# Silu of the expert gates as one ScalarE instruction, in an attention and expert block

## The reference

```python
h = _layernorm(x) * (1 + ca) + sa
x = x + ga * attention(h)                 # 16 heads, causal, content part 16 wide, rotary part 64 wide
h = _layernorm(x) * (1 + cb) + sb
# the experts, on h as x:
probs = softmax(x @ gate_weight.T)        # 32 experts
top_val, top_idx = top_k(probs, 8); top_val /= sum(top_val)
w_tg = weights of the top 8, summed by merge group (8 groups)
gate, up = split(einsum('th,goh->tgo', x, gate_up_proj[dominant_experts]))   # 96 wide for each group
act = jax.nn.silu(gate) * up
y = einsum('tgi,ghi->tgh', act, down_proj[dominant_experts])
out = einsum('tg,tgh->th', w_tg, y)
x = x + gb * out
```

## Time and profile before

| | |
|---|---|
| median of 3 runs | 1019.88 us (1019.28 to 1020.67) |
| the profiled execution | 1020.3 us, of which its span is 1018.6 |
| mean granted TensorE clock | 0.981 |
| PE busy | 962.8 us (95%) |
| PE weight loads busy | 704.9 us (69%) |
| DVE busy | 685.2 us (67%) |
| POOL busy | 496.8 us (49%) |
| ACT busy | 426.2 us (42%) |

### The profile page before, as it was taken

How to read it: one execution, slowest core, us unless ns; L and a number is a source line. 1 busy time by engine, 2 the same in 40 slices (tenths; PEclk the granted TensorE clock), 3 DMA queues, 4 the chain that set the end, 5 groups by cost and what they waited for, 6 DMA issues and landing times.

```text
span 1018.6 us, 23971 instructions
## 1 busy us (share of the span) xinstructions
PE 962.8 (95%) x9847; PEld 704.9 (69%) x9847; DVE 685.2 (67%) x1371; ACT 426.2 (42%) x780; POOL 496.8 (49%) x462
## 2 busy tenths in 40 slices
PE   5789999999999999999999999999999999998897
PEld 3546667766687677866777667866778667875566
DVE  5676767675776757667676758777576766766334
ACT  5234444264433634344442644245443445333332
POOL 2345454673545552663625644555526636356202
PEclk9889999999999999999999999999999999999999
DMA  6322010210102101200102101030002101011000
GB/s 205 81 87 84 33 62 2 75 63 2 63 1 95 43 11 53 73 33 33 63 2 73 64 2 63 7 99 33 33 33 73 49 17 63 1 53 64 2 1 21
DMA packets 37599, 48.73 MB, mean 48 GB/s; under 512 B 9386, under 2 KB 23210, under 8 KB 37490
## 3 DMA queue, kind: packets, MB, share of 16 engines
q1 hardware_dynamic: 37490, 47.20, 13.9%
HBM read 17.80 MB, written 4.21 MB: 22 GB/s over the span
## 4 chain that ended last, share of the span: by engine, by line
PE 75%; DVE 9%; ACT 6%; POOL 4%; issue 3%; DMA 2%; SPq 2%; POOLq 0%; DVEq 0%; ACTq 0%
PE ring L1206 15%; PE ring L1053 11%; PE ring L1054 9%; PE ring L1055 9%; PE ring L1178 7%; PE av L1222 7%; ACT pt L746 3%; DVE mcol L943 3%; PE ring L1283 2%; PE ring L1285 2%; PE ring L1284 2%; DVE prod L919 2%; PE ring L1190 2%; PE ring L1114 1%; SPq L537 1%
## 5 line engine op out<-in xcount | busy, mean ns | idle before, releaser
L746 ACT ACTIVATE pt<-ring 128x384 f32<-128x384 f32 (+1 forms) x384 | 171.0, 533 | 256.7 <-PE ring L1206 226.8
L943 DVE TENSOR_REDUCE mcol<-ring 128x1 f32<-128x128 f32 (+3 forms) x512 | 211.1, 482 | 47.8 <-PE ring L1183 47.2
L624 POOL TENSOR_SCALAR_AFFINE_SELECT pt<-pt 128x512 f32<-128x512 f32 x128 | 81.0, 646 | 215.4 <-ACT pt L746 215.4
L919 DVE TENSOR_TENSOR prod<-ring,table 128x1024 f32<-128x1024 f32 x128 | 154.5, 1217 | 44.4 <-PE ring L1055 40.1
L1206 PE MATMUL ring<-rows 32*128 32x512 f32 (+3 forms) x3072 | 172.2, 329 | 6.5 <-ACT pt L746 5.3
L1206 PEld LDWEIGHTS ring<-rows 32*128 32x128 f32 x3072 | 127.4, 184 | 53.4 <-issue 20.4
L597 POOL TENSOR_TENSOR rows<-prod,rows 128x1024 fp32r<-128x1024 f32 x64 | 152.6, 2390 | 17.3 <-ACT rows L725 16.4
L590 POOL TENSOR_TENSOR prod<-prod 128x512 f32<-128x512 f32 x64 | 82.0, 1281 | 87.2 <-DVE prod L919 86.6
L1178 PE MATMUL ring<-rows 32*128 32x512 f32 (+3 forms) x1024 | 89.9, 361 | 16.3 <-DMA cont<-h_lo 4.7
L725 ACT ACTIVATE rows<-prod 128x1024 fp32r<-128x1024 f32 x64 | 67.7, 1073 | 88.0 <-POOL prod L591 83.1
L1222 PE MATMUL av<-pt,vals 128*17 128x512 f32 (+3 forms) x1024 | 87.3, 447 | 4.3 <-POOL pt L624 4.3
(11 more groups left out here) (189 smaller groups left out, 1798.5 us busy)
## 6 DMA issues: line engine op xcount, KB each, us to landing
cont<-h_hi SPq DMA_DIRECT2D x96, 128.0 KB, 2.0
cont<-h_lo SPq DMA_DIRECT2D x96, 128.0 KB, 2.0
xn<-x_dram SPq DMA_DIRECT2D x8, 512.0 KB, 4.7
xr<-x_dram SPq DMA_DIRECT2D x8, 512.0 KB, 4.2
out_dram<-xr SPq DMA_DIRECT2D x8, 512.0 KB, 3.2
gate_bc<-gates_scratch SPq DMA_DIRECT2D x8, 256.0 KB, 4.4
pt<-wmod_dram SPq DMA_DIRECT2D x1, 1536.0 KB, 6.7
pt<-gup_t_dram SPq DMA_DIRECT2D x16, 96.0 KB, 2.5
```

What stands on the lines that cost most here:

```text
L746: sc.activation(pt[:, PT_AT[n] + h * w:PT_AT[n] + (h + 1) * w], ps[:, 0:w], ACT.Exp, scale=SCALE).then_inc(exp_ready.sem, 1)
L919: ve.tensor_tensor(prod[:, s % PROD, :, :], ps[:, :].unsqueeze(1).broadcast_to([P, 2, S]), table[:, :, :], ALU.mult).then_inc(rotated.sem, 1)
L943: last = ve.reduce_max(mcol[:, q, h * HR + ONE_ROW:h * HR + ONE_ROW + 1], ps[:, at:at + (q + 1) * P], AX_X)
```

## The change

ScalarE applies silu to the bank of gate and writes it to `inner`. The VectorE step `gated` is gone with its semaphore; the bank of gate is released by ScalarE, and `upped` is a plain product. The step keeps the name `tanh`. In both written orders all six of these steps now stand behind `ex.0`, and both orders are new throughout; `SETUP_ORDER` and the numbers of warm matmuls are the same.

```diff
@@ semaphores
-        tanh_ready = Count(sem("tanh_ready"), FT)
@@ ScalarE, kind == "tanh"
                         ps = wait_full(sc, b, part, ("gate", ahead, k))
-                        sc.activation(inner[:, k, :], ps[:, :], ACT.Tanh, scale=0.5).then_inc(tanh_ready.sem, 1)
+                        sc.activation(inner[:, k, :], ps[:, :], ACT.Silu).then_inc(gate_used.sem, 1)
@@ VectorE
-                    elif kind == "gated":
-                        k = step[2]
-                        wait(ve, tanh_ready, b, ahead, k)
-                        ps, act = bank(b, part, PLACES[part][0][("gate", ahead, k)]), inner[:, k, :]
-                        ve.scalar_tensor_tensor(act, act, 1.0, ps[:, :], ALU.add, ALU.mult)\
-                          .then_inc(gate_used.sem, 1)
                     elif kind == "upped":
...
-                        ve.scalar_tensor_tensor(act, act, 0.5, ps[:, :], ALU.mult, ALU.mult)\
-                          .then_inc(up_used.sem, 1)
+                        ve.tensor_tensor(act, act, ps[:, :], ALU.mult).then_inc(up_used.sem, 1)
@@ BODY_ORDER, the start
-rope.0200 score.000 rotate.0200 load_next.1 rope.0201 exp.000 loads.0 maxima.010 rotate.0201 clear.000 qcon.01
-reduce.010 combine.020 score.001 qcon_hi.01 qcon_lo.01 rope.0210 exp.001 maxima.011 rotate.0210 clear.001 rope.0211
-reduce.011 maxima.012 rotate.0211 value.000 reduce.012 combine.021 value.001 score.002 kcon.01 exp.002 shift.01
-rope.0300 kcon_hi.01 clear.002 hi.020 kcon_lo.01 rope.0301 shifted.01 move_k.02 hi.021 lo.020 stats1.1 value.002
+score.000 load_next.1 rope.0200 exp.000 rope.0201 rotate.0200 score.001 rotate.0201 clear.000 stats1.1 combine.020
+value.000 exp.001 maxima.010 rope.0210 reduce.010 clear.001 pow1.1 score.002 rotate.0210 rope.0211 exp.002 maxima.011
+rotate.0211 clear.002 value.001 reduce.011 combine.021 maxima.012 value.002 reduce.012 kcon.01 qcon.01 kcon_hi.01
+hi.020 kcon_lo.01 shift.01 qcon_hi.01 move_k.02 lo.020 rope.0300 shifted.01 hi.021 qcon_lo.01 score.010 move_q.02
...
@@ BODY_ORDER, the middle
-pow1.1 value.010 exp.011 maxima.020 combine.030 norm1.1 rope.0311 reduce.020 score.012 clear.011 rotate.0311
-maxima.021 combine.031 exp.012 move_q.03 maxima.022 hi.030 move_k.03 reduce.021 hi.031 clear.012 turn1.10 reduce.022
-turn1.11 lo.030 modulate1.10 value.011 modulate1.11 low1.10 shift.02 maxima.030 shifted.02 low1.11 value.012
-reduce.030 score.020 attn_out.01 score.021 exp.020 maxima.031 clear.020 exp.021 value.020 reduce.031 clear.021 lo.031
+attn_out.00 rotate.0300 rope.0301 exp.010 maxima.020 rotate.0301 norm1.1 clear.010 maxima.021 reduce.020 combine.030
+value.010 reduce.021 lo.021 maxima.022 rope.0310 reduce.022 score.011 rotate.0310 rope.0311 exp.011 turn1.10
+rotate.0311 clear.011 score.012 modulate1.10 combine.031 shift.02 exp.012 move_k.03 low1.10 turn1.11 shifted.02
+value.011 hi.030 loads.0 move_q.03 score.020 clear.012 modulate1.11 lo.030 hi.031 value.012 low1.11 score.021 exp.020
+attn_out.01 maxima.030 clear.020 exp.021 value.020 reduce.030 clear.021 lo.031 score.022 maxima.031 exp.022 value.021
...
@@ BODY_ORDER, the experts
-values_out.11 up.00 logits_copy.0 turn_l.0 gate.00 top.0 rotate.1110 up.01 tanh.00 rotate.1111 ex.0 gate.01 top2.0
-gate.02 tanh.01 gated.00 turn_w.0 gated.01 up.02 wT.0 upped.00 tanh.02 upped.01 gate.03 wT_lo.0 weigh.00 weigh.01
+rotate.1111 maxima.102 logits_copy.0 hi.110 combine.111 turn_l.0 reduce.102 up.00 gate.00 top.0 ex.0 up.01 top2.0
+gate.01 tanh.00 upped.00 turn_w.0 tanh.01 up.02 wT.0 upped.01 wT_lo.0 gate.02 weigh.00 weigh.01 weighed.00 up.03
...
@@ LAST_ORDER, the attention of group 1 and 2
-... exp.010 rope.0301 kcon_lo.01 move_k.02 score.011 attn_out.00 lo.021 rope.0310 rotate.0301 exp.011 maxima.020 clear.010 value.010 rotate.0310 combine.030 reduce.020 score.012 exp.012 rope.0311 maxima.021 rotate.0311 reduce.021 maxima.022 combine.031 clear.011 hi.030 clear.012 ...
+value.001 shifted.01 score.010 hi.020 move_k.02 clear.002 hi.021 lo.020 value.002 exp.010 attn_out.00 maxima.020
+rope.0300 reduce.020 clear.010 lo.021 score.011 rotate.0300 value.010 exp.011 maxima.021 clear.011 rope.0301
+reduce.021 score.012 rotate.0301 value.011 exp.012 move_q.03 maxima.022 move_k.03 rope.0310 clear.012 reduce.022
+combine.030 loads.0 rope.0311 rotate.0310 shift.02 value.012 shifted.02 hi.030 rotate.0311 score.020 attn_out.01
...
@@ LAST_ORDER, from the last exp
-... exp.032 clear.032 warm.00 value.031 value.032 warm.01 attn_out.03 wofold.0 mix.00 mix.01 warm.02 mixed.00 mixed.01 stats2.0 pow2.0 norm2.0 turn2.00 turn2.01 warm.03 modulate2.00 modulate2.01 low2.00 low2.01 logits.0 logits_copy.0 gate.00 turn_l.0 tanh.00 gate.01 tanh.01 gate.02 tanh.02 gated.00 up.00 up.01 top.0 gate.03 gated.01 gated.02 up.02 ex.0 tanh.03 upped.00 top2.0 gate.04 turn_w.0 wT.0 ...
+warm.01 clear.032 value.032 attn_out.03 mix.00 mix.01 mixed.00 warm.00 mixed.01 warm.02 stats2.0 pow2.0 norm2.0
+turn2.00 turn2.01 modulate2.00 warm.03 modulate2.01 low2.00 low2.01 logits.0 up.00 logits_copy.0 turn_l.0 gate.00
+top.0 ex.0 top2.0 gate.01 tanh.00 up.01 turn_w.0 gate.02 wT.0 tanh.01 wT_lo.0 gate.03 tanh.02 upped.00 weigh.00
+tanh.03 weigh.01 weighed.00 gate.04 upped.01 gate.05 tanh.04 weighed.01 inner_hi.00 inner_hi.01 inner_lo.00 up.02
+tanh.05 inner_lo.01 weigh.02 upped.02 up.03 up.04 weighed.02 upped.03 inner_hi.02 weigh.03 upped.04 weigh.04
+inner_lo.02 up.05 weighed.03 weighed.04 inner_hi.03 weigh.05 upped.05 down.00 inner_lo.03 weighed.05 inner_hi.04
+inner_lo.04 inner_hi.05 inner_lo.05 down.01 join.00 join.01 store.0
```

More of the change, by code:

```diff
@@ L94 @@
[L94 to L97, removed]
-values_out.10 rotate.1100 pow2.0 move_k.11 maxima.100 rotate.1101 norm2.0 maxima.101 reduce.100 combine.110 turn2.00
@@ L99 @@
-values.11 modulate2.00 reduce.101 turn2.01 lo.101 rope.1110 modulate2.01 low2.00 rope.1111 hi.110 low2.01 logits.0
-values_out.11 up.00 logits_copy.0 turn_l.0 gate.00 top.0 rotate.1110 up.01 tanh.00 rotate.1111 ex.0 gate.01 top2.0
-gate.02 tanh.01 gated.00 turn_w.0 gated.01 up.02 wT.0 upped.00 tanh.02 upped.01 gate.03 wT_lo.0 weigh.00 weigh.01
-weighed.00 up.03 gated.02 inner_hi.00 tanh.03 upped.02 gate.04 inner_lo.00 gated.03 weigh.02 tanh.04 gate.05 gated.04
-weighed.01 up.04 tanh.05 upped.03 inner_hi.01 weighed.02 inner_lo.01 weigh.03 upped.04 weigh.04 inner_hi.02 up.05
@@ L104 @@
-gated.05 inner_lo.02 weighed.03 weigh.05 weighed.04 inner_hi.03 maxima.102 upped.05 inner_lo.03 down.00 weighed.05
-inner_hi.04 reduce.102 inner_hi.05 inner_lo.04 inner_lo.05 lo.110 shift.10 join.00 down.01 combine.111 shifted.10
-hi.111 join.01 lo.111 store.0
+score.000 load_next.1 rope.0200 exp.000 rope.0201 rotate.0200 score.001 rotate.0201 clear.000 stats1.1 combine.020
+value.000 exp.001 maxima.010 rope.0210 reduce.010 clear.001 pow1.1 score.002 rotate.0210 rope.0211 exp.002 maxima.011
+rotate.0211 clear.002 value.001 reduce.011 combine.021 maxima.012 value.002 reduce.012 kcon.01 qcon.01 kcon_hi.01
@@ new lines @@
+attn_out.01 maxima.030 clear.020 exp.021 value.020 reduce.030 clear.021 lo.031 score.022 maxima.031 exp.022 value.021
+reduce.031 clear.022 maxima.032 wofold.0 latent.1 reduce.032 rope.1000 latent_hi.1 shift.03 value.022 shifted.03
+rotate.1000 score.030 latent_lo.1 attn_out.02 rope.1001 exp.030 score.031 rotate.1001 clear.030 combine.100 value.030
+exp.031 score.032 clear.031 rope.1010 exp.032 kcon.10 rotate.1010 clear.032 value.031 kcon_hi.10 hi.100 kcon_lo.10
+value.032 lo.100 qcon.10 attn_out.03 rope.1011 qcon_hi.10 qcon_lo.10 mix.00 rotate.1011 move_q.10 combine.101 mix.01
@@ L107 @@
+inner_hi.00 tanh.02 gate.03 inner_lo.00 hi.111 upped.02 weighed.01 lo.110 weigh.02 weigh.03 inner_hi.01 gate.04
+tanh.03 upped.03 weigh.04 tanh.04 up.04 weighed.02 inner_lo.01 weighed.03 inner_hi.02 gate.05 inner_lo.02 upped.04
+weighed.04 up.05 tanh.05 inner_hi.03 inner_lo.03 weigh.05 upped.05 shift.10 down.00 weighed.05 inner_hi.04 inner_lo.04
+inner_hi.05 inner_lo.05 lo.111 down.01 join.00 shifted.10 join.01 store.0
 """
 LAST_ORDER = """
[L110 removed]
@@ new lines @@
+maxima.010 qcon.01 reduce.010 score.000 qcon_hi.01 qcon_lo.01 rope.0200 exp.000 score.001 rotate.0200 clear.000
+value.000 exp.001 maxima.011 clear.001 rope.0201 reduce.011 maxima.012 rotate.0201 rope.0210 reduce.012 combine.020
+kcon.01 rope.0211 kcon_hi.01 rotate.0210 score.002 rotate.0211 kcon_lo.01 combine.021 shift.01 exp.002 move_q.02
+value.001 shifted.01 score.010 hi.020 move_k.02 clear.002 hi.021 lo.020 value.002 exp.010 attn_out.00 maxima.020
+rope.0300 reduce.020 clear.010 lo.021 score.011 rotate.0300 value.010 exp.011 maxima.021 clear.011 rope.0301
```

9 lines of the change are left out of this document (6 added, 3 removed).

## The result

The changed kernel takes 1037.15 us (median of 4 runs, 1034.95 to 1039.81) where the kernel before took 1019.58 beside it: ratio 1.0173, interval 1.0147 to 1.0200. Measured again later beside other runs it was 1.0181 [1.0158, 1.0204]. The forecast was 1018.4 with a range of 1010 to 1026; the kernel is slower by 18 us, outside the range. The profiled run took 1039.81, its span 1038.1.

The account below looks back on a forecast made before the run. PE bounds the kernel (busy 962.8 of 1018.6 us), so a VectorE step counts only where PE waits. Terms -2.4 - 2.0 + 0.9 + 3.0 + 0.5 - 1.5 = -1.5 us give 1018.4 us from 1019.88; range 1010 to 1026.

Parts of the forecast that it names:

- Batches 1 to 6: Whole order changes there; -0.25 us a batch, -1.5 in all, with bounds of -1.2 and +1.0 a batch.
- The walk: Step-by-step pass through the new body with batch 3's starts and lengths, giving 117.85 us without a low spell.
- first rival: DVE waits for xn in every batch, delaying score.002: 1.2 us x 6 batches, 1025.6 us; chance 20%.
- The undisturbed batch: New body without a low clock spell: 117.85 us, its large stalls changing places.
- Batch 0: stats1.1 ahead of reduce.010 waits for late xn: +3.0 us, bounds 1 and 4.5; another +0.5 for the order.
- The load ahead of exp.000: Table load on idle ACT at each batch's start, not held by exp.000's wait, so hidden: 0 us.
- the third rival: Load ahead of exp.000 exposed, score.001 having 1.5 us slack: 1 us x 7 gives 1025.4 us; chance 6%.
- Last batch: Sum for the last batch under its new order: tail -2.4, attention -2.0, warm matmuls and clock +0.9 us.
- The tail: End of last batch: inner_lo steps start earlier, down.00 takes 4.35 us for 6.93; gain 2.4, bounds 1.3 and 2.6.
- The attention: Last batch up to mix.00: value.011's wait for clear.011 goes, new stalls come; gain 2.0 us, bounds 0 and 4.
- The warm matmuls: Last batch: PE idles 2.4 us before mix.00, so the low spell comes at the mixes; +0.9, bounds -0.6 and +1.5.
- The exchange itself: Silu for tanh and gated, in the expert stage where PE has no gap: nothing on PE's path.

Follow-up runs that it names:

- e12: Changed kernel with loads.0 moved from ahead of move_q.03 to behind value.022 in the body order: 1032.91 us, 1.0134 of the kernel before.
- e8: Changed kernel with exp.020 ahead of hi.031 on ScalarE in the body order: 1039.62 us, 1.0203 of the kernel before.
- e3: Changed kernel with stats1.1 put back behind shifted.01 and pow1.1 ahead of clear.010: 1041.03 us, 1.0231 of the kernel before.
- e7: Changed kernel with a one-element Exp behind the last inner_hi in the bodies (early table load): 1035.02 us, 1.0149 of the kernel before.
- e9: e7 with stats1.1 moved behind rotate.0210 and pow1.1 behind clear.002: 1033.67 us, 1.0156 of the kernel before.
- e16: Changed kernel with loads.0 behind value.022 and stats1.1 behind rotate.0210, without the early table load: 1025.28 us, 1.0050 of the kernel before.
- e15: Changed kernel with loads.0 behind value.022 and the early table load, stats1.1 not moved: 1028.89 us, 1.0098 of the kernel before.
- e13: Changed kernel with loads.0 behind value.022, the early table load and stats1.1 behind rotate.0210: 1024.36 us, 1.0061 of the kernel before.
- e6: e2 with a one-element Exp behind the last inner_hi in the bodies (early table load): 1016.34 us, 0.9975 of the kernel before.
- e2: Changed kernel (silu, no gated) on the old orders, with tanh.00 to .02 moved behind ex.0: 1022.32 us, 1.0027 of the kernel before.

## Why the prediction was wrong

**Batches 1 to 6: forecast -1.5, came +10.3 us. This step failed, and it is most of the error.** Two terms were put at nothing. The first is the transfer. The walk went through PE's waits for ACT, DVE and POOL with durations of batch 3, and has no longer landing for any move of h_hi and h_lo. loads.0 moves from the start of the body to right ahead of move_q.03 on SP's queue. The prediction saw that it had left its old place (against its first rival) and never costed it at the new one, where 768 KB go ahead of moves that PE waits for. e12 puts 4 to 5 us on it. The premise was thin as well: in before, 24 of 192 moves already took more than 2.4 us, up to 4.4, most of them with a packet of the instruction queue under way.

The second is the clock. The walk's 117.85 is a batch without a low spell, set against an average of 118.1 that had four in six batches. The new order has four again, 13.7 us in batches 1 to 6, worth 6.8 us at half its length. The six batches exceed six times 117.85 by 11.8 us: 6.8 is this clock, 0.9 the undisturbed batch (118.0), and the other 4.1 are longer waits. By the walk the large stalls change places, and the forecast gave no reason why the spells behind them should go. The bound of +1.0 a batch held for the undisturbed ones and not for those with the collision.

**The undisturbed batch: right in size.** The walk's 117.85 came out as 118.0, where an undisturbed batch of before takes 117.1. Of its stalls, maxima.021 has 1.1 us (0.7 forecast), maxima.022 0.5 (0.8), maxima.031 0.9 (0.6), maxima.101 1.1 (0.75) and score.021 1.5 (1.4). The cause given for score.021 was wrong in the main (e8): exp.020 waits for value.012.

**Batch 0: forecast +3.5, came +8.4.** The mechanism of stats1.1 was right: it waits for xn until 80.2, and reduce.010's second head was free at 83.37 where the forecast was 83.6. Its size was right too once the clock is taken out. In the four pairs of kernels that differ by the place of stats1.1 alone, batch 0 shortens by 5.6 us (after to e3), 4.8 (e7 to e9), 6.3 (e12 to e16) and 3.4 (e15 to e13). With half of the time at the lower level taken off, these are 2.9 to 3.9, where the forecast had 3.0. Two other terms were missing. rope.0200 no longer fills PE's wait at the end of setup, 1.9 us. And the lower clock holds 10.2 us of the batch, 3.4 before, worth 3.4. The prediction said that batch 0 of before lost nothing to a low spell after its start; the trace has one there, from 74.3 to 77.7, clock 0.57 over 74 to 78.

**The load ahead of exp.000: forecast 0, bounds 0 and 1.28 a batch.** The reason given was wrong. The earlier trace rows showed a load that ran while an ACTIVATE waited, but that ACTIVATE was the first of the program; where the load serves an activation that waits for a semaphore, it came behind the wait in all 7 places. On the old orders e6 against e2 puts 5.3 us on it, inside the bounds. In the bodies of the changed kernel 0 was nearly right, and not because the load is hidden: score.001 takes 1.72 to 1.78 us in batches 1 to 6, 1.67 to 1.69 before, so the slack that the third rival named takes most of it up. In the last batch it costs 1.3. ScalarE: Activation LUTs in the Trainium skill (What ACT_TABLE_LOAD costs) gives 1283 ns for the load and a drain besides, about 2.66 us in all. In the traces here the activation starts 0.01 us behind a load of 1.28, at 15 of the 16 loads of after (the first waits for a DMA), and e6 has loads 0.02 us behind the activation ahead of them; so they speak against the larger figure.

**Last batch: forecast -3.5, came +0.8.** The tail was right: down.00 takes 4.86 us (1023.83 to 1028.69), forecast 4.35, before 6.93; the stage is 2.15 shorter, forecast 2.4. The attention gains nothing (71.51 us against 70.90, forecast 2.0 less): it has the clock of 1.00 that was forecast, but score.001 lost 1.3 us behind the load ahead of exp.000, maxima.020 waits for 1.3 where before has no such wait, and score.021 has a stall of 1.9 (0.9 before). maxima.032 has the 1.6 that was forecast; shift.03 and score.031 stall for 1.2 and 1.5 us in both kernels. The warm matmuls did what was forecast, in excess:

```profile
986.50 3.75 PE L1241 MATMUL av<-xn,room 128*128 128x256 f32 x8 [2.42 <-DVE room L981]
990.05 3.20 PE L1241 MATMUL ring<-xn,room 128*128 128x256 f32 x8
```

The two mixes took 3.6 and 2.9 us from start to start instead of 1.8 and 1.5, right behind 2.42 us of idle, and the low spell was 6.8 us long, not 3.4; mix.00 to the end of logits is 2.35 us longer, forecast 0.9.

**The exchange itself: forecast 0, right.** PE has no gap in the expert stage; e6 puts silu without its exposed load at -0.25% [-0.42, -0.07] on the old orders. Rival 1 came on DVE and not on PE: the prediction's sign for it, idle before stats1.1 in every batch, is there with 0.3 to 1.1 us in batches 1 to 6 (3.3 in all, beside 4.9 in batch 0), and of the score.002 of these batches only that of batch 4 is longer, by 0.4 us. Its evidence left out one load of before that took 5.8 us.

**What stays open.** e13 is still 0.9% behind e6, which differs by the orders alone: 0.5 us in batch 0, 1.0 in each of batches 1 to 6, and 3.0 at the start of batch 0: 1.8 is rope.0200, and score.000 itself starts 1.2 later. No single step stands out, and no run splits this rest further. e9 is open too: the same move of stats1.1 that gains in e16 gave nothing that could be measured there.

## What to carry to other kernels

When an order is rewritten, list the transfers too: for each DMA that moves, what is issued within the next few us behind it on its queue and who waits for that. Compare like with like: a walk without low spells stands against a batch without them, and the spells are a term of their own, to be kept unless the stalls go. Give each table load the place at which the engine has nothing to do by a small activation there, since otherwise it stands behind the semaphore of the work that it serves; but behind the last step that somebody waits for. And a step that costs nothing in the steady batches can cost 3 us and more in the first one, where its input is late or where it no longer fills a wait of setup.

## What the runs showed of the hardware

- The load of a table lands behind the wait of the activation that needs it: 7 of 7 ahead of exp.000 in after, 1.28 us each, ACT idle 9.2 us before six of them and 1.75 before the last.
- Most moves of 128 KB land in 1.9 to 2.1 us (median 2.0 in before). Issued right behind 768 KB they took 2.6 to 4.5 in after. Elsewhere some took up to 4.4 (24 of 192 above 2.4 in before), 17 of these 24 with a packet of the instruction queue between issue and landing.
- The same stall isn't the same in every batch: with one order batches 4 and 6 took 4.8 and 2.7 us more than batch 5, and a spell of 3.4 us at clock 0.5 followed the stall at maxima.030 each time, worth half its length. Once the moves landed early (e12), neither had it; stalls of 0.8 and 0.7 us at maxima.100 and .101 had a spell behind them in batches 3 and 4 of after, and those of 1.1 and 0.7 us in batch 1 had none.
- A spell at the lower clock was 6.8 us long behind 2.42 us of idle at the mixes, 3.4 in most other places.
